# The down product of expert tiles as three products of high and low parts, made one tile later

## The chip, the cores and the metric

The kernel runs on one core of one Trainium2 chip, in one launch. The metric is the device time of that launch in microseconds (us), lower is better; a figure for a kernel is the median of its runs.

The engines of a core that matter here: TensorE (PE: matrix products; PEld is its weight loads, which overlap the products), VectorE (DVE), ScalarE (ACT), GpSimd (POOL) and SyncE (SP), which only issues transfers. Each works through its own list of instructions in order and stops at a semaphore until another engine, or a transfer that lands, has counted it up. So an instruction that waits holds back all that stands behind it on its engine.

## The reference, cut to what matters

A layer of four residual steps on 1024 tokens of 512 numbers, all in fp32: a state-space mixer, a mixture-of-experts block, a block-sparse product, and the same mixture-of-experts block again. Only the two expert blocks are touched:

```
g, u = split(x2 @ shared_w_gate_up.T);  shared_out = silu(g) * u @ shared_w_down.T
probs = softmax(x2 @ gate_w.T);  the best 2 of 16 experts per token, weights normed
gu  = einsum('th,eih->eti', x2, w_gate_up)      # 512 -> 2 * 128 per expert
act = silu(g) * u
out_e = einsum('eti,ehi->eth', act, w_down)     # 128 -> 512 per expert
out = sum over the 2 experts of out_e * combine + shared_out
```

## The kernel before, in words

The expert block runs twice (`run` 0 and 1). Each run computes the shared expert as two halves (`first`, `second`) over all tokens; between the two halves stands **the tile loop**, which this change is about. The 2048 pairs of token and expert are sorted by expert into slots, 128 slots to a tile. `TILES = 31` is the most tiles that any routing can need, and all 31 are always worked through. `own[tau]` in memory says which expert tile `tau` belongs to.

What one tile needs, by engine (names as the profile has them; a tile of memory may be seen under the name of the larger buffer that it lies in):

- SyncE loads gate and up weights (`tgu`, 512 KB, a ring of `GU_RING = 4`, seen as `mem<-wffn_d` L565) and down weights (`tdn`, 256 KB, a ring of `DN_RING = 3`, seen as `mem` or `spare<-wffn_d` L574). For both it first reads the expert's number from `own` into a register. It also stores the finished tile (`tile_out`, `slots_y<-quad`, 256 KB, L579).
- GpSimd gathers the tile's token rows (`cv<-xn_dram,toks`, L750), up to 256 KB; slots that are empty bring nothing.
- TensorE turns the rows (`t_rows`, L1917, 4 transposes), makes gate and up (`t_gate_up`, L1930, 8 products 128x128 by 128x128, plain fp32), and makes down (`t_down`, L1942, one product 128x128 by 128x512, plain fp32). The trace shows a plain fp32 product as two records.
- ScalarE takes the tanh of the gate (`t_tanh`, L1050), copies the turned rows out of PSUM (`t_rows_evac`, L1044) and copies the finished tile out of PSUM (`t_out`, `quad<-bank`, L1057), which counts up `ty_ok`.
- VectorE makes the hidden activations from tanh, gate and up (`t_hidden`, L1546 and L1548), into `thid`, a ring of `H_RING = 3`, seen as `E`.

The orders are written out by hand, one list to an engine, in steps of `k`. The list that matters most is SyncE's:

```
for k in range(TILES + 1):
    if k + GU_RING < TILES:
        tile_gate_up(run, k + GU_RING)
    if DN_RING <= k - 1 + DN_RING < TILES:
        tile_down(run, k - 1 + DN_RING)
    if k:
        tile_out(run, k - 1)
```

So in step `k` SyncE issues the gate-and-up load of tile `k+4`, the down load of tile `k+2`, and the store of tile `k-1`. The store waits for `ty_ok` of tile `k-1`.

Elsewhere (the mixer, the shared halves) products are already made from high and low parts: a value is copied to `fp32r`, a shorter form, as its high part, the difference goes to a second `fp32r` buffer, and `three` (L1627 through its helper) adds high by high, high by low and low by high in one bank. The buffers are `ah`, `al` for activations and `wh`, `wl` for weights.

Of the kernel before, what the change touches and what calls it, by code (L numbers as in the profile page):

```python
# [17 lines left out]
P = 128  # L18
TT = TOK // P
# [6 lines left out]
TILES = 2 * TOK // P + EXPERTS - 1  # L26
GU_RING, DN_RING, X_RING, Y_RING, H_RING = 4, 3, 4, 4, 3
# [6 lines left out]
def hybrid_layer(nc, x_d, wconv_d, wgate_d, wout_d, wdt_d, cpar_d, gpar_d, dtb_d, alog_d,  # L34
# [3 lines left out]
    ALU = mybir.AluOpType  # L38
    ACT = mybir.ActivationFunctionType
# [3 lines left out]
    with ctx:  # L43
        def sb(name, shape, dt=f32):
            return ctx.enter_context(nc.sbuf_tensor(name, shape, dt))

        def sem(name):
            return ctx.enter_context(nc.semaphore(name))
# [7 lines left out]
        wh = sb("wh", [P, 11, HID], f32r)  # L56
        wl = sb("wl", [P, 11, HID], f32r)
        ah = sb("ah", [P, 2, 4, P], f32r)
        al = sb("al", [P, 2, 4, P], f32r)
# [16 lines left out]
        thid = [E[:, 0, P * q:P * q + P] for q in range(H_RING)]  # L76
# [16 lines left out]
        tdn = [mem[:, 4096:4608], mem[:, 4608:5120], spare[:, HID:2 * HID]]  # L93
# [48 lines left out]
        bank = [ctx.enter_context(nc.psum_tensor(f"bank{n}", [P, HID], f32)) for n in range(8)]  # L142
# [65 lines left out]
        def counted(name, n):  # L208
            s = sem(name)
            per[name] = (s, n)  # L210
            return name
# [68 lines left out]
        dn_mm = counted("dn_mm", TT)  # L280
# [13 lines left out]
        td_in = [sem(f"td_in{q}") for q in range(DN_RING)]  # L294
        tx_in = [sem(f"tx_in{q}") for q in range(X_RING)]
        ty_out = [sem(f"ty_out{q}") for q in range(Y_RING)]
        ga_in = [sem(f"ga_in{t}") for t in range(TT)]
        tx_mm, tx_ok = sem("tx_mm"), sem("tx_ok")
        tg_mm, tg_th, tg_hg, tg_h = sem("tg_mm"), sem("tg_th"), sem("tg_hg"), sem("tg_h")
        ty_mm, ty_ok, cmb = sem("ty_mm"), sem("ty_ok"), sem("cmb")  # L300
        YB = (5, 6)
        DN_BANKS = ((4, 6, 7), (4, 5, 6, 7))

        def inc(instr, name, n=1):
            instr.then_inc(per[name][0], n)

        def now(eng, name, i, n):

            eng.wait_ge(per[name][0], per[name][1] * (i + 1) + n)

        def before(eng, name, i, n):

            eng.wait_ge(per[name][0], per[name][1] * i + n)
# [141 lines left out]
        def hidden_rows(i, j, low):  # L455
# [3 lines left out]
            s = (10, 0)[j - 2] if i % 2 else 7 + j  # L459
            return (wl if low else wh)[:, s, :].rearrange("p (a b) -> p a b", a=4)  # L460

        def job(run, tau):

            return run * TILES + tau

        def uses(ring, run, tau):

            return run * len(range(tau % ring, TILES, ring)) + tau // ring + 1
# [4 lines left out]
        def _(sp):  # L473
# [93 lines left out]

            def tile_down(run, tau):
                if tau >= DN_RING:
                    sp.wait_ge(ty_mm, job(run, tau - DN_RING) + 1)  # L570
                elif run:
                    sp.wait_ge(ty_mm, TILES)
                e = sp.value_load(own[0:1, tau:tau + 1], min_val=0, max_val=EXPERTS - 1)
                sp.dma_start(tdn[tau % DN_RING], experts[bass.ds(e, 1), :, 2, :].rearrange("e p n -> p (e n)")  # L574
                             ).then_inc(td_in[tau % DN_RING], 16)
# [216 lines left out]
        def _(act):  # L792
# [4 lines left out]
            def step(instr):  # L797
                steps[0] += 1
                instr.then_inc(act_step, 1)
                return steps[0]  # L800
# [168 lines left out]
            for b in range(BATCH):  # L969
                bs = slice(b * SEQ, (b + 1) * SEQ)  # L970
                act.wait_ge(pe_step, b + 1)
                n = step(nc.scalar.activation(v_hm[:, bs], bank[(DG, ST)[b]][:, :], ACT.Identity, bias=dtb[:, 0:1]))
                act.wait_ge(act_step, n)
                n = step(nc.scalar.activation(u_hm[:, bs], v_hm[:, bs], ACT.Abs))
# [53 lines left out]
            def hidden(i, j):  # L1028
                now(act, g_mm, i, j + 1)
                if j >= 2:  # L1030
                    now(act, a_lo, i, j - 1)
                else:
                    before(act, a_lo, i, 3 + j)
                inc(nc.scalar.activation(gt[:, j % 2, :], bank[j % 2][:, :], ACT.Tanh, scale=0.5), f_th)
                now(act, f_h, i, j + 1)
                before(act, dn_mm, i, TT)
                inc(nc.scalar.activation(hidden_rows(i, j, 0), gt[:, j % 2, :].rearrange("p (a b) -> p a b", a=4),
                                         ACT.Copy), a_hi)
# [7 lines left out]
            def t_tanh(run, tau):  # L1046
                act.wait_ge(tg_mm, job(run, tau) + 1)
                if tau >= H_RING:
                    act.wait_ge(ty_mm, job(run, tau - H_RING) + 1)
                nc.scalar.activation(thid[tau % H_RING], bank[2 + tau % 2][:, 0:P], ACT.Tanh,  # L1050
                                     scale=0.5).then_inc(tg_th, 1)

            def t_out(run, tau):
                act.wait_ge(ty_mm, job(run, tau) + 1)
                if tau >= Y_RING:
                    act.wait_ge(ty_out[tau % Y_RING], 16 * uses(Y_RING, run, tau - Y_RING))
                nc.scalar.activation(ybuf[tau % Y_RING], bank[YB[tau % 2]][:, :], ACT.Copy).then_inc(ty_ok, 1)  # L1057

            for run in range(2):
                if run == 1:  # L1060
                    layer_norm(2)
                    layer_norm(3)
                act.wait_ge(rt_dve, run * 3 + 2)
                nc.scalar.activation(pr[:, :, :], pr[:, :, :], ACT.Exp).then_inc(rt_dve, 1)
                first, second = 2 * run, 2 * run + 1
                act.wait_ge(rt_tr, run + 1)
                for j in range(4):
                    hidden(first, j)
                for k in range(-2, TILES + 1):
                    if 0 <= k < TILES:  # L1070
                        t_tanh(run, k)
                    if k + 2 < TILES:
                        t_rows_evac(run, k + 2)
                    if 0 <= k - 1:
                        t_out(run, k - 1)
                    if 1 <= k <= 4:
                        w_part(second, k - 1)
                    if run == 0 and 11 <= k <= 14:
                        if k == 11:
                            act.wait_ge(sp_ok, 1)  # L1080
                        nc.scalar.activation(wh[:, k - 5, :], wsp[:, k - 11, :], ACT.Copy).then_inc(sp_hi, 1)
                    if 20 <= k <= 21:
                        w_part(second, k - 16)
                for j in range(4):
                    hidden(second, j)
# [3 lines left out]
        def _(dve):  # L1089
# [11 lines left out]
            TS, STT, TTn = nc.vector.tensor_scalar, nc.vector.scalar_tensor_tensor, nc.vector.tensor_tensor  # L1101
# [277 lines left out]
            for run in range(2):  # L1379
# [162 lines left out]
                def t_hidden(tau):  # L1542
                    n = job(run, tau) + 1
                    dve.wait_ge(tg_th, n)
                    hid = thid[tau % H_RING]
                    STT(hid, hid, 1.0, bank[2 + tau % 2][:, 0:P], ALU.add, ALU.mult).then_inc(tg_hg, 1)  # L1546
                    dve.wait_ge(tg_hg, n)
                    TTn(hid, hid, bank[2 + tau % 2][:, P:2 * P], ALU.mult).then_inc(tg_h, 1)  # L1548

                first, second = 2 * run, 2 * run + 1  # L1550
                hidden_gate(first, 0)
# [66 lines left out]
        def _(pe):  # L1618
            mm = nc.tensor.matmul
            credit(pe, (big_mm, tr_mm, st_mm, off_mm, diag_mm, ss_mm, out_half, g_mm, u_mm, dn_mm))  # L1620

            def three(out, hi, lo, w_hi_, w_lo_, first, last, data_left):

                pairs = ((hi, w_hi_), (hi, w_lo_), (lo, w_hi_)) if data_left else \
                    ((w_hi_, hi), (w_hi_, lo), (w_lo_, hi))
                for n, (l, r) in enumerate(pairs):
                    got = mm(out, l, r, start=first and n == 0, stop=last and n == 2)  # L1627
                return got
# [174 lines left out]
            for run in range(2):  # L1803
# [33 lines left out]
                if run == 0:  # L1837
# [3 lines left out]
                       start=True, stop=True).then_inc(pe_step, 1)  # L1841
# [91 lines left out]
                    last.then_inc(tg_mm, 1)  # L1933

                def t_down(tau):
                    pe.wait_ge(tg_h, job(run, tau) + 1)
                    pe.wait_ge(td_in[tau % DN_RING], 16 * uses(DN_RING, run, tau))
                    if tau >= 2:
                        pe.wait_ge(ty_ok, job(run, tau - 2) + 1)
                    else:  # L1940
                        now(pe, dn_acc, 2 * run, TT)
                    mm(bank[YB[tau % 2]][:, :], thid[tau % H_RING], tdn[tau % DN_RING], start=True,  # L1942
                       stop=True).then_inc(ty_mm, 1)

                first, second = 2 * run, 2 * run + 1
                for n, (what, a, b) in enumerate(FFN_ORDER):
# [10 lines left out]
                        tokens()  # L1957
                for tau in range(2):
                    t_rows(tau)
                for k in range(TILES + 1):  # L1960
                    if k < TILES:
                        t_gate_up(k)
                    if k + 2 < TILES:
                        t_rows(k + 2)
                    if k:
                        t_down(k - 1)
                for what, a, b in FFN_ORDER:
                    if what == "gu":
                        gate_up(second, a, b, 0)
# [65 lines left out]
```

## Time and profile before

| | us |
|---|---|
| median of 3 runs | 2027.59 (2026.63 to 2031.39) |
| the profiled execution, its time | 2021.97 |
| its span, first to last instruction | 2020.1 |
| PE busy | 1966.5 (97%) |
| DVE busy | 1504.9 (74%) |
| ACT busy | 1181.0 (58%) |
| POOL busy | 1034.4 (51%) |
| mean granted clock of TensorE, full speed is 1 | 0.993 |

How to read it: a share of busy time is a mean over stages with different limits. The tile loop runs twice, from about 1669 to 1765 us and from about 1886 to 1981 us of the span. "idle before, releaser" is the time in which an engine stood still before an instruction, and what ended it. The clock 1.00 is 2.4 GHz, 0.50 is 1.2 GHz.

### The profile page before, as it was taken

The numbers are of one execution on the slowest core, as the hardware profiler recorded it, in microseconds if no ns is written. First come the engines' busy times: TensorE is split into PE (matmuls) and PEld (weight loads), VectorE is DVE, ScalarE is ACT, GpSimd is POOL, SyncE is SP. The second block draws the span as 40 slices with busy tenths as digits, with TensorE's granted clock in tenths as the row PEclk, the third lists the DMA queues.
The fourth block names the chain that finished last, engine by engine and source line by source line (L and its number), as shares of the span: only waits on it lengthen the run. The fifth ranks groups of instructions, "written<-read, shape, count | busy, mean of one in ns | idle before, by whom it ended". The sixth has DMA issues, their size and how long they took to land.

```text
span 2020.1 us, 38785 instructions
## 1 busy us (share of the span) xinstructions
PE 1966.5 (97%) x11776; PEld 1634.7 (81%) x11776; DVE 1504.9 (74%) x2838; ACT 1181.0 (58%) x2570; POOL 1034.4 (51%) x907
## 2 busy tenths in 40 slices
PE   5999999999999999999999999999999989998998
PEld 4888888888888888888888888888888868876887
DVE  7998599859976997699679967985899572176315
ACT  4785388538843874497449645963696335432442
POOL 1497059616941793279228823981497025250433
PEclk8999999999999999999999999999999999999999
DMA  2552145214512351334134313530352049931896
GB/s 101 160 169 56 49 120 168 57 45 121 162 47 74 111 147 43 92 113 127 43 92 135 111 38 97 150 101 28 107 162 83 21 138 379 340 114 42 310 378 199
DMA packets 143910, 253.95 MB, mean 126 GB/s; under 512 B 21448, under 2 KB 37832, under 8 KB 143696
## 3 DMA queue, kind: packets, MB, share of 16 engines
q1 hardware_dynamic: 134848, 231.35, 36.7%
q0 software_dynamic: 7520, 16.80, 2.7%
q10 hardware_dynamic: 1328, 3.15, 0.4%
q8 instruction: 111, 1.82, 0.4%
q14 instruction: 103, 0.84, 0.1%
HBM read 233.38 MB, written 25.69 MB: 128 GB/s over the span
## 4 chain that ended last, share of the span: by engine, by line
PE 90%; DVE 6%; ACT 1%; issue 1%; POOL 0%; DMA 0%; DVEq 0%; ACTq 0%; SPq 0%
PE bank L1627 60%; PE bank L1739 7%; PE bank L1930 6%; PE bank L1753 5%; PE bank L1693 4%; PE bank L1942 3%; PE bank L1721 2%; PE bank L1917 1%; DVE Y L1230 1%; DVE spare L1318 1%; PE bank L1712 1%; PE bank L1760 1%; PE bank L1635 1%; DVE Y L1239 1%; POOL wl L743 0%
## 5 line engine op out<-in xcount | busy, mean ns | idle before, releaser
L1627 PE MATMUL bank<-xh,wh 128*128 128x512 f32 x1288 | 523.4, 406 | 10.7 <-POOL wl L713 4.0
L1627 PE MATMUL bank<-xh,wl 128*128 128x512 f32 x1288 | 504.4, 392 | 0.0
L1627 PE MATMUL bank<-xl,wh 128*128 128x512 f32 x1288 | 502.2, 390 | 0.0
L713 POOL TENSOR_TENSOR wl<-raw,wh 128x512 fp32r<-128x512 f32 x144 | 192.8, 1344 | 460.8 <-ACT wh L861 460.8
L1230 DVE SCALAR_TENSOR_TENSOR Y<-bank,cpar,Y 128x511 f32<-128x511 f32 (+2 forms) x384 | 286.8, 747 | 24.4 <-ACT Y L905 15.4
L1627 PEld LDWEIGHTS bank<-xh,wh 128*128 128x128 f32 x1288 | 242.9, 189 | 60.6 <-POOL wl L713 4.9
L1627 PEld LDWEIGHTS bank<-xh,wl 128*128 128x128 f32 x1288 | 242.0, 188 | 54.2
L1627 PEld LDWEIGHTS bank<-xl,wh 128*128 128x128 f32 x1288 | 243.2, 189 | 45.5 <-issue 0.5
L730 POOL TENSOR_TENSOR Y<-Y,gt 128x512 f32<-128x512 f32 x128 | 184.9, 1444 | 94.5 <-DVE gt L1284 92.8
L1292 DVE TENSOR_TENSOR al<-Y,ah 128x512 fp32r<-128x512 f32 x128 | 95.6, 747 | 169.1 <-ACT ah L963 169.1
L1627 PE MATMUL bank<-wh,ah 128*128 128x512 f32 x544 | 213.7, 393 | 2.8 <-DVE X L1539 2.2
L1627 PE MATMUL bank<-wh,al 128*128 128x512 f32 x544 | 211.9, 389 | 0.0
L1627 PE MATMUL bank<-wl,ah 128*128 128x512 f32 x544 | 211.7, 389 | 0.0
L963 ACT ACTIVATE ah<-Y 128x512 fp32r<-128x512 f32 x128 | 80.6, 630 | 212.0 <-PE bank L1627 212.0
L937 ACT ACTIVATE gt<-bank 128x512 f32<-128x512 f32 x128 | 76.4, 597 | 165.7 <-PE bank L1627 97.9
L680 POOL TENSOR_TENSOR Y<-Y,E 128x384 f32<-128x384 f32 x128 | 136.3, 1065 | 44.6 <-DVE E L1261 44.6
L925 ACT ACTIVATE mem<-mem,hpt 128x128 f32<-128x128 f32 x512 | 156.2, 392 | 0.0
L905 ACT ACTIVATE Y<-bank,cpar 128x512 f32<-128x512 f32 x128 | 99.2, 775 | 96.3 <-PE bank L1627 95.4
L750 POOL DMA_INDIRECT cv<-xn_dram,toks x62 | 63.0, 1017 | 173.7 <-DVE own L1479 89.6
L706 POOL TENSOR_TENSOR mem<-mem,quad 128x512 f32<-128x512 f32 x112 | 143.7, 1307 | 0.0
L692 POOL TENSOR_TENSOR mem<-mem,hpt 128x384 f32<-128x384 f32 x128 | 107.3, 839 | 66.6 <-DVE mem L1198 61.3
L1546 DVE SCALAR_TENSOR_TENSOR E<-E,bank 128x128 f32<-128x128 f32 x62 | 17.8, 288 | 153.2 <-ACT E L1050 145.1
(232 smaller groups left out, 4072.0 us busy)
## 6 DMA issues: line engine op xcount, KB each, us to landing
mem<-c_rows SPq DMA_DIRECT2D x128, 256.0 KB, 3.8
mem<-wffn_d SPq DMA_DIRECT2D x62, 512.0 KB
E<-e_rows SPq DMA_DIRECT2D x256, 96.0 KB, 3.4
raw<-wconv_d SPq DMA_DIRECT2D x80, 256.0 KB, 3.0
cv<-c_rows SPq DMA_DIRECT2D x64, 256.0 KB, 3.9
spare<-c_rows SPq DMA_DIRECT2D x64, 256.0 KB, 4.2
raw<-wgate_d SPq DMA_DIRECT2D x64, 256.0 KB, 2.7
raw<-wout_d SPq DMA_DIRECT2D x64, 256.0 KB, 2.6
```

What stands on the lines that cost most here:

```text
L680: inc(pool.tensor_tensor(dst, dst, E[:, u % ER, :], ALU.add), y_ok)
L692: inc(pool.tensor_tensor(xd[:, u % 2, :, :].rearrange("p c (h d) -> p c h d", d=HD), xs[:, u % 3, 0:CH - 1, :].rearrange("p c (h d) -> p c ...
L706: inc(pool.tensor_tensor(L[n % LR], L[n % LR], G[:, b * CH:(b + 1) * CH, :].rearrange("p c i -> p (c i)"), ALU.mult), lg_ok)
L713: inc(pool.tensor_tensor(wl[:, W_SLOT[p], :], raw[:, R_SLOT[p], :], wh[:, W_SLOT[p], :], ALU.subtract), w_lo)
L730: inc(pool.tensor_tensor(dst, dst, gt[:, n % 2, :], ALU.mult), y_gated)
L905: inc(nc.scalar.activation(dst, bank[big_bank(i, k)][:, :], ACT.Identity, scale=cpar[:, tile, TAPS - 1:TAPS], bias=cpar[:, tile, TAPS:TAPS ...
L925: last = nc.scalar.activation(L[n % LR][:, c * P:(c + 1) * P], L[n % LR][:, c * P:(c + 1) * P], ACT.Relu, scale=-1.0, bias=hp[:, b * CH + ...
L1230: last = STT(dst[:, s:SEQ], bank[big_bank(i, k)][:, 0:SEQ - s], cpar[:, tile, TAPS - 1 - s:TAPS - s], dst[:, s:SEQ], ALU.mult, ALU.add)
L1627: got = mm(out, l, r, start=first and n == 0, stop=last and n == 2)
L1739: last = mm(b4(DG)[hs, c, :], xs[:, u % 3, c, hs], L[(2 * u + h) % LR][:, c * P:(c + 1) * P], start=True, stop=True)
L1753: last = mm(b4(OF)[:, c, :], S[:, u % 2, c, :], CT[:, t * P:(t + 1) * P], start=True, stop=True)
L1930: last = mm(bank[2 + tau % 2][:, a * P:(a + 1) * P], tgu[tau % GU_RING][:, a, kt * P:(kt + 1) * P], xT[tau % 2][:, kt, :], start=kt == 0, ...
```

## The change

The down product of a tile becomes three products of high and low parts, as elsewhere in the kernel. For this

- ScalarE copies the down weights of the tile to `ah` (`t_down_hi`) and the hidden activations to `wh` (`t_hid_hi`), both `fp32r`;
- VectorE subtracts these from the full values into `al` and `wl` (in `t_hidden`, counted by `td_lo` and `th_lo`);
- TensorE makes `t_down` of tile `k-2` in step `k`, where before it made that of tile `k-1`; ScalarE's `t_out` moves from tile `k-1` to tile `k-2` in step `k` likewise, behind the two new copies;
- SyncE's down load waits for `td_lo` in place of `ty_mm`. SyncE's order stays as it was.

```
+            def t_down_hi(run, tau):
+                act.wait_ge(td_in[tau % DN_RING], 16 * uses(DN_RING, run, tau))
+                if tau < 2:
+                    now(act, dn_mm, 2 * run, TT)
+                else:
+                    act.wait_ge(ty_mm, job(run, tau - 2) + 1)
+                nc.scalar.activation(down_rows(tau, 0), tdn[tau % DN_RING], ACT.Copy).then_inc(td_hi, 1)
+
+            def t_hid_hi(run, tau):
+                act.wait_ge(tg_h, job(run, tau) + 1)
+                nc.scalar.activation(hid_rows(tau, 0), thid[tau % H_RING], ACT.Copy).then_inc(th_hi, 1)
...
-                for k in range(-2, TILES + 1):
+                for k in range(-2, TILES + 2):
                     if 0 <= k < TILES:
                         t_tanh(run, k)
+                        t_down_hi(run, k)
+                        t_hid_hi(run, k)
                     if k + 2 < TILES:
                         t_rows_evac(run, k + 2)
-                    if 0 <= k - 1:
-                        t_out(run, k - 1)
+                    if 0 <= k - 2:
+                        t_out(run, k - 2)
...
                     TTn(hid, hid, bank[2 + tau % 2][:, P:2 * P], ALU.mult).then_inc(tg_h, 1)
+                    dve.wait_ge(td_hi, n)
+                    TTn(down_rows(tau, 1), tdn[tau % DN_RING], down_rows(tau, 0), ALU.subtract).then_inc(td_lo, 1)
+                    dve.wait_ge(th_hi, n)
+                    TTn(hid_rows(tau, 1), hid, hid_rows(tau, 0), ALU.subtract).then_inc(th_lo, 1)
...
                 def t_down(tau):
-                    pe.wait_ge(tg_h, job(run, tau) + 1)
-                    pe.wait_ge(td_in[tau % DN_RING], 16 * uses(DN_RING, run, tau))
+                    pe.wait_ge(th_lo, job(run, tau) + 1)
...
-                    mm(bank[YB[tau % 2]][:, :], thid[tau % H_RING], tdn[tau % DN_RING], start=True,
-                       stop=True).then_inc(ty_mm, 1)
+                    three(bank[YB[tau % 2]][:, :], hid_rows(tau, 0), hid_rows(tau, 1), down_rows(tau, 0),
+                          down_rows(tau, 1), True, True, True).then_inc(ty_mm, 1)
...
-                for k in range(TILES + 1):
+                for k in range(TILES + 2):
                     if k < TILES:
                         t_gate_up(k)
                     if k + 2 < TILES:
                         t_rows(k + 2)
-                    if k:
-                        t_down(k - 1)
+                    if k >= 2:
+                        t_down(k - 2)
...
                 if tau >= DN_RING:
-                    sp.wait_ge(ty_mm, job(run, tau - DN_RING) + 1)
+                    sp.wait_ge(td_lo, job(run, tau - DN_RING) + 1)
```

How it stands in ScalarE's list, before: a little over one step of the tile loop once its rings are full (`E<-bank` is the tanh, `hpt` or `spare<-bank` the turned rows, `quad<-bank` the finished tile, which counts up `ty_ok`).

```order
L1050 ACTIVATE E<-bank 128x128 [waits ty_mm,tg_mm]
L1044 ACTIVATE hpt<-bank 128x512 [waits tg_mm,tx_mm]
L1057 ACTIVATE quad<-bank 128x512 [waits ty_out1,ty_mm]
L1050 ACTIVATE E<-bank 128x128 [waits ty_mm,tg_mm]
L1044 ACTIVATE spare<-bank 128x512 [waits tg_mm,tx_mm]
L1057 ACTIVATE quad<-bank 128x512 [waits ty_out2,ty_mm]
```

And ScalarE's list of the change at the same place (`ah<-` is the copy of the down weights, `wh<-E` that of the hidden activations).

```order
L1059 ACTIVATE E<-bank 128x128 [waits th_lo,tg_mm]
L1068 ACTIVATE ah<-mem 128x512 [waits ty_mm,td_in1]
L1072 ACTIVATE wh<-E 128x128 [waits tg_h]
L1053 ACTIVATE spare<-bank 128x512 [waits tg_mm,tx_mm]
L1078 ACTIVATE quad<-bank 128x512 [waits ty_out1,ty_mm]
```

The wait for the down load (`td_in`) now stands on ScalarE, ahead of the copy that counts up `ty_ok`; before it stood on TensorE.

SyncE's list in the tile loop, of the change, from one store to the next (`slots_y<-quad` is the store, L571 and L580 read the expert's number).

```order
L586 DMA slots_y<-quad 128x512 [waits ty_ok]
L571 TENSOR_LOAD own [waits tg_mm]
L571 ISA x2
L572 ISA
L572 DMA mem<-wffn_d 128x2x512
L580 TENSOR_LOAD own [waits td_lo]
L580 ISA x2
L581 ISA
L581 DMA spare<-wffn_d 128x512
L586 DMA slots_y<-quad 128x512 [waits ty_ok]
```

Nothing moved in it; the down load waits for `td_lo` where it waited for `ty_mm`, and it still stands behind the store and the gate-and-up load.

## Rows read from the trace of the kernel before

**Rows 1.** Page: span, busy time by engine, clock and DMA share in 40 slices.

```profile
span 2020.1 us, 38785 instructions
...
PE 1966.5 (97%) x11776; PEld 1634.7 (81%) x11776; DVE 1504.9 (74%) x2838; ACT 1181.0 (58%) x2570; POOL 1034.4 (51%) x907
...
PEclk8999999999999999999999999999999999999999
DMA  2552145214512351334134313530352049931896
```

**Rows 2.** Chain that ended last, 1700 to 1712 us: start, duration, what.

```profile
1700.90 0.44 PE bank L1917 x4
1701.34 0.86 PE bank L1942 x2
1702.20 1.78 PE bank L1930 x16
1703.98 0.44 PE bank L1917 x4
```

**Rows 3.** Groups by line, 1668 to 1765 us: busy, mean ns, idle before.

```profile
L1942 PE MATMUL bank<-mem,E 128*128 128x512 f32 x42 | 21.7, 598 | 0.6 <-issue 0.4 <-DVE E L1548 0.2
L1057 ACT ACTIVATE quad<-bank 128x512 f32<-128x512 f32 x31 | 18.5, 597 | 9.6 <-PE bank L1942 9.6
...
L1942 PE MATMUL bank<-spare,E 128*128 128x512 f32 x20 | 10.2, 594 | 0.0
L1044 ACT ACTIVATE hpt<-bank 128x512 f32<-128x512 f32 x16 | 9.6, 597 | 11.4 <-PE bank L1917 11.2 <-issue 0.2
...
L1548 DVE TENSOR_TENSOR E<-E,bank 128x128 f32<-128x128 f32 x31 | 8.9, 287 | 1.1
L1050 ACT ACTIVATE E<-bank 128x128 f32<-128x128 f32 x31 | 8.6, 278 | 32.6 <-PE bank L1930 29.8 <-issue 2.8
...
L1019 ACT ACTIVATE wh<-raw 128x512 fp32r<-128x512 f32 x6 | 3.7, 622 | 0.0
```

**Rows 4.** Stretches of the loop: PE, PEld, DVE, ACT, POOL busy, clock, DMA.

```profile
1690.00:1720.00 30.00, 30.00 (x218) 25.56 (x218) 5.43 (x19) 16.24 (x34) 19.91 (x16) 1.00 1.04 396
1720.00:1750.00 30.00, 29.55 (x210) 24.70 (x209) 5.47 (x20) 15.35 (x31) 11.57 (x11) 1.00 1.04 385
1750.00:1765.00 15.00, 14.85 (x98) 11.59 (x98) 2.87 (x10) 6.21 (x14) 0.00 (x0) 1.00 0.72 262
```

**Rows 5.** Chain that ended last: a stretch of products of parts.

```profile
1660.63 7.14 PE bank L1627 x30
```

**Rows 6.** Page: VectorE's subtraction of a high part, 128x512.

```profile
L1292 DVE TENSOR_TENSOR al<-Y,ah 128x512 fp32r<-128x512 f32 x128 | 95.6, 747 | 169.1 <-ACT ah L963 169.1
```

**Rows 7.** Timeline of SyncE's queue, a little over one step.

```profile
1700.67 0.33 SPq L574 DMA_DIRECT2D spare<-wffn_d  x1
1701.05 0.43 SPq L579 DMA_DIRECT2D slots_y<-quad  x1
1702.23 0.38 SPq L565 DMA_DIRECT2D mem<-wffn_d  x1
1703.66 0.33 SPq L574 DMA_DIRECT2D mem<-wffn_d  x1
```

**Rows 8.** Page: DMA issues, KB each, median us from issue to landing.

```profile
spare<-c_rows SPq DMA_DIRECT2D x64, 256.0 KB, 4.2
raw<-wgate_d SPq DMA_DIRECT2D x64, 256.0 KB, 2.7
```

**Rows 9.** Timeline: a down load issued, and the product of that tile.

```profile
1726.37 0.34 SPq L574 DMA_DIRECT2D mem<-wffn_d  x1
...
1729.70 0.33 SPq L574 DMA_DIRECT2D spare<-wffn_d  x1
...
1732.60 1.10 PE L1942 MATMUL bank<-mem,E 128*128 128x512 f32 x2 [0.45 <-issue]
```

**Rows 10.** Stretches of 1 us outside the loop, columns as in rows 4.

```profile
1798.00:1799.00 1.00, 0.00 (x0) 0.00 (x0) 0.96 (x4) 0.00 (x0) 0.00 (x0) 1.00 0.00 0
1799.00:1800.00 1.00, 0.45 (x4) 0.45 (x5) 1.00 (x3) 0.93 (x2) 0.00 (x0) 1.00 0.00 0
1801.00:1802.00 1.00, 0.55 (x3) 0.55 (x4) 1.00 (x3) 0.55 (x2) 0.00 (x0) 0.73 0.00 0
1802.00:1803.00 1.00, 1.00 (x7) 1.00 (x5) 1.00 (x2) 0.40 (x1) 0.00 (x0) 0.50 0.00 0
1805.00:1806.00 1.00, 1.00 (x6) 0.84 (x5) 0.97 (x3) 1.00 (x3) 1.00 (x2) 1.00 0.00 0
```

More of the change, by code:

```diff
@@ L298, in hybrid_layer @@
         tx_mm, tx_ok = sem("tx_mm"), sem("tx_ok")
+        td_hi, td_lo, th_hi, th_lo = sem("td_hi"), sem("td_lo"), sem("th_hi"), sem("th_lo")
         tg_mm, tg_th, tg_hg, tg_h = sem("tg_mm"), sem("tg_th"), sem("tg_hg"), sem("tg_h")
@@ L460, in hidden_rows, with down_rows, hid_rows @@
             return (wl if low else wh)[:, s, :].rearrange("p (a b) -> p a b", a=4)
+        def down_rows(tau, low):
+            return (al if low else ah)[:, tau % 2, :, :].rearrange("p a b -> p (a b)")
+        def hid_rows(tau, low):
+            return (wl if low else wh)[:, 10, tau % 2 * P:(tau % 2 + 1) * P]
         def job(run, tau):
@@ L569, in tile_down @@
                 if tau >= DN_RING:
-                    sp.wait_ge(ty_mm, job(run, tau - DN_RING) + 1)
+                    sp.wait_ge(td_lo, job(run, tau - DN_RING) + 1)
                 elif run:
-                    sp.wait_ge(ty_mm, TILES)
+                    sp.wait_ge(td_lo, TILES)
                 e = sp.value_load(own[0:1, tau:tau + 1], min_val=0, max_val=EXPERTS - 1)
@@ L1035, in hidden @@
                 now(act, f_h, i, j + 1)
+                if i % 2:
+                    act.wait_ge(ty_mm, job(i // 2, TILES))
                 before(act, dn_mm, i, TT)
@@ L1048, in t_tanh @@
                 if tau >= H_RING:
-                    act.wait_ge(ty_mm, job(run, tau - H_RING) + 1)
+                    act.wait_ge(th_lo, job(run, tau - H_RING) + 1)
                 nc.scalar.activation(thid[tau % H_RING], bank[2 + tau % 2][:, 0:P], ACT.Tanh,
                                      scale=0.5).then_inc(tg_th, 1)
+            def t_down_hi(run, tau):
[8 more added lines that the diff above has]
+                nc.scalar.activation(hid_rows(tau, 0), thid[tau % H_RING], ACT.Copy).then_inc(th_hi, 1)
             def t_out(run, tau):
```

## The prediction

> **What bounds the kernel now.** I read the page first: TensorE is busy 97% of the span, and the digits of the DMA line are high in only two places [rows 1]. These two places are the tile loops, and only they are changed, so the rest of the kernel is taken as it was. Inside the loop I read the chain of work that ended last: it is TensorE alone, and it repeats 0.44 us of turned rows, 0.86 us of down product and 1.78 us of gate and up [rows 2]. That is **3.08 us a tile**, and the row of the next transposes (1703.98 against 1700.90) says the same. TensorE is busy 30.00 of 30 us there [rows 4]. So before, TensorE sets the loop. But the transfers are full as well: the DMA share is 1.04 at 396 and 385 GB/s, and drops to 0.72 only where no more loads are issued [rows 4]. ScalarE has room: it is busy 16.24 of 30 us, 1.7 of 3.08 a tile, and most of what it waits for is TensorE [rows 3, 4].
>
> Third, SyncE's queue. From a store (L579, 1701.05) to the next gate-and-up load (L565, 1702.23) it takes 1.18 us, to the next down load (L574, 1703.66) 2.61 us; from that down load to the one before (1700.67) it is 2.99 us [rows 7]. Hardly any of this is waiting: it is reading the expert's number and building the transfer. SyncE needs about 3.0 of the 3.08 us of a tile. It has no room for being held up.
>
> **The change part by part.** *TensorE.* A down product was 0.86 us [rows 2]. Thirty products of parts, 128x512, ran in 7.14 us, 0.238 each [rows 5], so three are 0.71 and a tile's work on TensorE falls to 2.93 us, by 0.15. The Trainium skill, "FP8 and Floating Point Precision", TensorE Precision Notes, has true fp32 as four passes through the array; by that, three passes in place of four would save a quarter, 0.21 us a tile. It changes nothing in what follows, where TensorE does not set the pace.
>
> *ScalarE.* Two copies come: 128x512 to `fp32r` at 0.62 (as L1019), and 128x128 at 0.28 (as L1050) [rows 3]. With tanh 0.28, rows 0.60 and out 0.60 a tile is 2.38 us: under 2.93, so ScalarE is no bound by its work.
>
> *VectorE.* A subtraction 128x512 at 0.75 [rows 6] and one of 128x128 at 0.29 [rows 3] join 0.58 us: 1.6 us a tile, no bound.
>
> *The waits.* This is what decides. ScalarE's `t_down_hi(k)` now waits for the down load of tile k, and `t_out(k-2)`, which counts up `ty_ok`, stands behind it in the same step. SyncE's store of tile k-2 waits for that `ty_ok`, and behind the store stand the gate-and-up load of k+4 and the **down load of k+2**. That load in turn is what ScalarE waits for two steps later. The store of tile k used to be released in ScalarE's step k+1; now it is in step k+2, but SyncE's order was not moved with it. So there is a ring over two steps:
>
> - ScalarE, from the landing of the down load to `ty_ok`: 0.62 + 0.28 + 0.60 + 0.60 = 2.10 us [rows 3];
> - SyncE, from the store to the issue of the down load: 2.6 us [rows 7];
> - the transfer, from issue to landing: not shown by itself for this load. From below, a load of 256 KB where the transfers are lightly used lands 2.7 us after issue; another kind of 256 KB takes 4.2 [rows 8]. From above, in the loop: the load issued at 1726.37 is that of the product at 1732.60, which waited 0.45 us for something that no engine had left open (the other load, issued at 1729.70, is the next tile's). That is 6.2 us [rows 9], at a DMA share of 1.04. After the change the same bytes move in some 4.5 us in place of 3.08, so the share falls to about 0.7, that of the end of the loop [rows 4]. I take 4.2, between the two ends and nearer the light one, since 512 KB were issued 1.4 us ahead on the same queue;
> - three hand-overs by semaphore (landing to ScalarE, to SyncE, SyncE to its queue): 0.2 us, an estimate.
>
> The sum is 2.1 + 2.6 + 4.2 + 0.2 = 9.1 us for two steps, **4.55 us a tile** against 3.08. It is TensorE that then waits, for `th_lo` and the rows that ScalarE gives out late.
>
> The Trainium skill, "DMA: Bandwidth & Descriptors", Anatomy of one DMA, fits a transfer that GpSimd issues as about 2.0 us plus its bytes at 436 GB/s. For 256 KB that is an estimate of 2.6 us, and the ring would be 7.5 us and the tile 3.75. The 6.2 us of the loop before disagree, since loads queue there.
>
> *How many tiles.* The down loads of tiles 0 to 2 are issued ahead of the loop, that of 3 ahead of the first store. Tiles 4 to 30 are bound: 27 a run. In the last two SyncE has no gate-and-up load to issue (1.2 us less), but the last product now comes about as much later behind ScalarE's copies: even. So 27 x (4.55 - 3.08) = 39.7 us a run, **79 us** for two. The profiled execution took 1.9 us more than its span, 2022.0 in all; 2022.0 + 79 = 2101. The median of the runs shown is 5.6 us above that execution, so on their scale it is 2027.6 + 79 = **2107 us**, 3.9% slower.
>
> TensorE's saving of 0.15 x 62 = 9 us lies under the ring and gives nothing. Other SyncE waits are no issue: `td_lo` of k-1 is long counted when the load of k+2 comes up, and the gate-and-up load has a ring of four and over two steps to land.
>
> *Bounds.* With a landing of 2.7 us the ring is 7.6, the tile 3.8, and the sum 27 x 0.72 x 2 = 39 us: 2066. With 6.2 us it is 11.1, 5.55 and 133 us: 2161.
>
> **Rivals.**
>
> 1. *Short landing.* The light share lets the load land in 2.7 to 3.3 us: 2066 to 2083. For it: the 2.7 of [rows 8]. Against it: the 512 KB just ahead, and gathers. The fit on the DMA page of the Trainium skill is on this side. Chance 0.17, and 0.04 for something shorter still, 2034 to 2066.
> 2. *Long landing, or a slow clock.* TensorE will now stand still for up to 2 us at a time. Outside the loop, after two slices of 1 us with TensorE busy 0.00 and 0.45, the granted clock fell from 1.00 to 0.50, that is from 2.4 to 1.2 GHz [rows 10]. If the whole loop ran at 1.2 GHz, TensorE would need 2 x 2.93 = 5.9 us a tile, above the ring, and the loss would be 2.8 x 27 x 2 = 150 us: 2178. Against it: a loop that is full at 1.2 GHz gives the clock no reason to stay there (at 1802 to 1803 TensorE was busy 1.00, and at 1805 the grant was 1.00 again [rows 10]), and a spell of a few us costs less than the 3 us that TensorE has over in two steps. With a landing above 5.2 us this side is 2134 to 2175. Chance 0.12.
> 3. *Faster: no ring.* If the down load still lands before ScalarE asks for it, TensorE stays the bound at 2.93 us: 2027.6 - 9 = 2018. It decides at the point where the ring comes under two tiles of TensorE, 5.9 us; 2.1 + 2.6 + 0.2 alone are 4.9, so the load would have to land within 1.0 us of its issue. The shortest 256 KB shown takes 2.7 [rows 8]. It can only be if ScalarE's or SyncE's list is not held as I read it. Chance 0.06.
> 4. *Same.* The ring is missing and SyncE's own 3.0 us, or the full transfers, take TensorE's gain: 2022 to 2033. Chance 0.03.
>
> **How the numbers follow.** The likeliest case, a landing of 3.3 to 5.2 us, gives 2083 to 2134 and has 0.58. The range of 2060 to 2150 takes in it, rival 1 and the near half of rival 2, and leaves out about 0.19. A difference of 0.3%, 6 us, is about what a measurement of this kernel can tell from no change. Faster 0.06, same 0.03, slower 0.91.
>
> **What would show it.** In the profile of the changed kernel each tile loop is some 40 us longer. TensorE is busy some 65% of it and the DMA share falls from 1.04 to about 0.7. ScalarE's `ah<-mem` and `ah<-spare` (L1068) have the longest idle time before them in the loop, 1.5 us a tile or more, with a transfer (or nothing that shows) as releaser. SyncE's stores (L586) wait for `quad` L1078 in every step, and a down load (L581) follows its store by 2.6 us. Tiles come in pairs, a long and a short one, since the ring goes over two steps. The rest of the kernel is as long as before. I am wrong if stores are issued without a wait, if L1068 never waits for its load, or if the clock line shows 0.5 through the loop.

## The result and the profile after

The changed kernel takes **2092.84 us** (2087.6 to 2095.91, 4 runs) against 2029.49 of the kernel before in the same comparison. The ratio is 1.0314 with a 95% interval of 1.0296 to 1.0332: 3.1% slower, +63 us. The prediction was 3.9%, +79 us on the same base, with a range that holds the result.

The span of the profiled execution is 2090.5 us, 70.4 more than [rows 1]. First, the page: busy time of the engines, the clock and the DMA share in 40 slices.

```profile
span 2090.5 us, 39219 instructions
...
PE 1983.0 (95%) x11838; PEld 1653.1 (79%) x11838; DVE 1554.3 (74%) x2962; ACT 1213.1 (58%) x2694; POOL 1034.2 (49%) x907
...
PEclk8999999999999999999999999999999999999999
DMA  2552135124313530352144134313520498614984
```

VectorE is 49 us busier than in [rows 1] and ScalarE 32, both well below the span: the added time is waiting. The stretches of the loop show whose (columns as in [rows 4]):

```profile
1690.00:1720.00 30.00, 23.70 (x179) 20.67 (x178) 11.15 (x30) 14.93 (x38) 13.53 (x10) 1.00 0.89 294
1720.00:1750.00 30.00, 21.15 (x153) 17.78 (x152) 9.99 (x27) 15.31 (x38) 11.55 (x11) 1.00 0.89 284
```

TensorE was busy 30.00 and 29.55 of 30 us in [rows 4]; now it is 23.70 and 21.15. The transfers are slower too, 294 GB/s for 396. ScalarE is busy half the time. All of them wait, so none of them is the bound by its work; what they wait for has to be read. The view of one line's instructions shows what ScalarE's new copy of the down weights (L1068) waits for, over both runs (us, times):

```profile
  DMA mem<-wffn_d: 76.6, 36
  DMA spare<-wffn_d: 32.7, 16
  PE bank L1654: 2.9, 3
```

That is 109 us in 52 of 62 tiles, for the down load. And SyncE's waits show its store (L586) behind ScalarE's out (L1078):

```profile
SPq L586 <- ACT quad L1078: 88.4, 56, 3.3
```

In the kernel before, the same wait was `SPq L579 <- ACT quad L1057: 8.8, 6, 2.3`. The chain that ended last, once round the ring (start, duration, what), of the kernel after:

```profile
1704.76 0.25 issue
1705.01 0.29 ACT wh L1072
1705.30 0.48 ACT hpt L1053
1705.79 0.49 ACT quad L1078
1706.30 0.33 SPq L586
...
1707.42 0.39 SPq L572
...
1708.75 0.06 SPq L581
...
1708.91 3.96 DMA mem<-wffn_d
...
1713.43 0.29 ACT wh L1072
1713.72 0.48 ACT hpt L1053
1714.21 0.50 ACT quad L1078
1714.72 0.33 SPq L586
...
1716.97 3.88 DMA mem<-wffn_d
```

Read it as a circle: out (L1078) counts up `ty_ok`, the store (L586) follows in 0.02 us, then the gate-and-up load (L572) and the down load (L581) are issued, the down weights land 3.96 us later, and ScalarE's copies lead to the next out. From the landing at 1712.87 to the store at 1714.72 is 1.85 us; from store to load 2.61 us (1706.30 to 1708.91) or 2.25 (1714.72 to 1716.97); the transfer is 3.9 to 4.0. Together 8.0 to 8.4 us, for two tiles. (In this and other kernels single loads differ; where sizes are compared below, the median of the down loads is used that stand in the chain between 1685 and 1765 and between 1935 and 2015 us. Here it is 4.07 us, of 18.) TensorE, which was the whole chain in [rows 2], does not stand in this cut. It does not vanish from the chain altogether: from 1722 to 1738 the view takes it through four steps of TensorE (gate and up, rows, down) and ScalarE. In these steps L1068 still waited 1.6 to 2.2 us for its load, and tiles came every 4.1 to 4.3 us, so the ring of loads is as long there.

The timeline of ScalarE gives the pace, by the starts of L1068 (the first line is tile 3, the last tile 30):

```profile
1682.76 0.63 ACT L1068 ACTIVATE ah<-mem 128x512 fp32r<-128x512 f32 x1 [0.97 <-DMA mem<-wffn_d]
1688.16 0.63 ACT L1068 ACTIVATE ah<-mem 128x512 fp32r<-128x512 f32 x1 [2.92 <-DMA mem<-wffn_d]
1691.01 0.63 ACT L1068 ACTIVATE ah<-spare 128x512 fp32r<-128x512 f32 x1 [0.37 <-DMA spare<-wffn_d]
1696.21 0.63 ACT L1068 ACTIVATE ah<-mem 128x512 fp32r<-128x512 f32 x1 [3.23 <-DMA mem<-wffn_d]
1699.54 0.63 ACT L1068 ACTIVATE ah<-mem 128x512 fp32r<-128x512 f32 x1 [1.37 <-DMA mem<-wffn_d]
...
1793.42 0.63 ACT L1068 ACTIVATE ah<-mem 128x512 fp32r<-128x512 f32 x1 [1.80 <-DMA mem<-wffn_d]
```

The first steps alternate, 5.4, 2.85, 5.2, 3.3 us, since the ring goes over two steps and odd and even tiles are two chains; between 1717 and 1742 us the steps are even, 3.9 to 4.4 us. From tile 3 to tile 30 it is 110.7 us, **4.10 us a tile** against 3.08.

### The profile page after: what moved, and what is told of

It reads as the page before. It is cut to its first block, busy times and chain, and to the rows that moved or that the text cites. A ratio compares the mean times of both kernels' runs of the same rounds, so it can differ in the third digit from the quotient of the medians.

```text
span 2090.5 us, 39219 instructions
## 1 busy us (share of the span) xinstructions
PE 1983.0 (95%) x11838; PEld 1653.1 (79%) x11838; DVE 1554.3 (74%) x2962; ACT 1213.1 (58%) x2694; POOL 1034.2 (49%) x907
## 4 chain that ended last, share of the span: by engine, by line
PE 80%; DVE 6%; DMA 5%; ACT 3%; issue 3%; SPq 2%; another core or an unknown queue 0%; DVEq 0%; POOL 0%; ACTq 0%
PE bank L1654 59%; PE bank L1766 6%; PE bank L1780 5%; PE bank L1720 4%; DMA mem<-wffn_d 3%; PE bank L1748 2%; DMA spare<-wffn_d 2%; DVE Y L1253 1%; PE bank L1957 1%; DVE spare L1341 1%; PE bank L1739 1%; PE bank L1787 1%; PE bank L1662 1%; SPq L580 1%; SPq L572 1%
## 5 line engine op out<-in xcount | busy, mean ns | idle before, releaser
L1241 DVE SCALAR_TENSOR_TENSOR mem<-mem,hpt,bank 128x64 f32<-128x64 f32 x512 | 121.0, 278 | 9.1
```

The lines of the kernel that those rows point to most:

```text
L1241: last = STT(S[:, u % 2, c, hs], S[:, u % 2, c - 1, hs], hp[:, b * CH + c, 3, 2 * pair + h:2 * pair + h + 1], so[:, c, hs], ALU.mult, ALU.add)
```

## The experiments

Eleven kernels ran, in three groups; each is compared with the kernel before on the same chip (its median was 2030.6, 2026.1 and 2027.6 us in the three).

**SyncE's store one step later.** The change moved the store's release by one step and left SyncE's list. Here the list follows.

```
-                for k in range(TILES + 1):
+                for k in range(TILES + 2):
...
-                    if k:
-                        tile_out(run, k - 1)
+                    if k >= 2:
+                        tile_out(run, k - 2)
```

> The changed kernel, with SyncE's store moved one step later too (tile k-2 in step k). Theory 'ring' (load of the down weights -> ScalarE's copy -> out -> store -> next down load, over two steps, 8.3 us): the ring now goes over three steps, 8.3 to 9.7 us by whether a load takes 4.0 or 5.5 us, so 2.93 (TensorE) to 3.2 us a tile, and the time is 2020 to 2038 us. Rival 'copies': ScalarE's and VectorE's added work slows the loop by itself; then the time stays at 2085 or more. Rival 'late load': the down weights are now wanted two steps before the product and a ring of 3 buffers with full transfers can't bring them; then the tile stays above 3.6 us, 2057 us or more.

Measured: 2036.81 us, ratio 1.0029 (1.0010 to 1.0047). Three numbers in SyncE's list take back 57 of the 63 us, and the result lies in the ring's range. ScalarE's and VectorE's added work is all still there, so the rival "copies" falls, and so does "late load" in the form in which it was given. The store's waits are down to a third:

```profile
SPq L586 <- ACT quad L1078: 29.9, 31, 2.2
```

**The store two steps later.** The same edit with 3 in place of 2.

> The changed kernel, with SyncE's store two steps later (tile k-3 in step k). Theory 'ring': the ring goes over four steps and can't bind; what is left is TensorE at 2.93 us, SyncE at about 3.0, or the transfers at 1.25 MB over 0.4 MB/us, 3.1 us: 2018 to 2031 us, no slower than with one step. Rival 'late load': 2057 us or more, as with one step. Rival 'copies': 2085 or more.

Measured: 2029.38 us, ratio 0.9996 (0.9985 to 1.0008): level with the kernel before, and the best form with the full loads. A stretch of its loop:

```profile
1690.00:1720.00 30.00, 28.52 (x215) 25.37 (x214) 16.55 (x36) 20.48 (x50) 19.65 (x16) 1.00 1.03 383
```

The DMA share is back at 1.03, and TensorE still waits 1.5 of 30 us.

**The down load first.** The store stays where the change has it; in a step SyncE issues the down load ahead of the gate-and-up load.

```
+                    if DN_RING <= k - 1 + DN_RING < TILES:
+                        tile_down(run, k - 1 + DN_RING)
                     if k + GU_RING < TILES:
                         tile_gate_up(run, k + GU_RING)
-                    if DN_RING <= k - 1 + DN_RING < TILES:
-                        tile_down(run, k - 1 + DN_RING)
```

> The changed kernel, with SyncE issuing the down load ahead of the gate-and-up load in a step; the store stays where it was. Theory 'ring': from store to down load it is 1.1 us in place of 2.25, and 512 KB less stand in front of the load, so it lands in 3.2 to 4.0 us: the ring is 6.2 to 7.0 us, 3.1 to 3.5 us a tile, 2030 to 2052 us. Rival 'copies': no change, 2085 to 2100. Rival 'late load': a load that is issued 1.1 us earlier gains 1.1 us in each step at most once, so 2075 or more.

Measured: 2069.19 us, ratio 1.0185 (1.0160 to 1.0209). The sign was right, the size was not, and 2069 is outside what any of the three had said. The chain shows which term was off:

```profile
1719.33 0.33 SPq L586
...
1720.43 0.33 SPq L581
```

and its next loads:

```profile
1712.42 5.06 DMA mem<-wffn_d
...
1724.51 4.50 DMA mem<-wffn_d
```

SyncE's term shrank as expected, from 2.25 or 2.6 us to 1.1. The transfer did not get shorter; it got longer: the median is 4.50 us, of 12, for 4.07. The expectation had "512 KB less in front of the load". That holds within a step, but the gate-and-up load of the step before still stands in front, as these rows of the timeline show (the first four are tile 21, the last three tile 29, behind which no gate-and-up load follows):

```profile
1745.79 0.38 SPq L572 DMA_DIRECT2D mem<-wffn_d  x1
1749.81 0.33 SPq L581 DMA_DIRECT2D mem<-wffn_d  x1
1750.91 0.38 SPq L572 DMA_DIRECT2D mem<-wffn_d  x1
1752.47 0.63 ACT L1068 ACTIVATE ah<-mem 128x512 fp32r<-128x512 f32 x1 [0.53 <-DMA mem<-wffn_d]
...
1775.20 0.38 SPq L572 DMA_DIRECT2D mem<-wffn_d  x1
1776.86 0.33 SPq L581 DMA_DIRECT2D spare<-wffn_d  x1
1781.79 0.63 ACT L1068 ACTIVATE ah<-spare 128x512 fp32r<-128x512 f32 x1 [2.17 <-DMA spare<-wffn_d]
```

Tile 21's load, 4.0 us behind the last gate-and-up load and with the next one 1.1 us behind it, landed within 2.66 us. Tile 29's, 1.66 us behind a gate-and-up load and with none behind it, took 4.93. Over both loops, among the loads that ScalarE waited for and that have the next gate-and-up load 0.9 to 1.6 us behind them, those issued at most 2.0 us after one have a median of 4.9 us (18 loads), those issued 3.0 us or more after one 3.1 us (13 loads). So the landing goes with how closely a large load stands ahead.

**Out first.** SyncE's list is untouched; on ScalarE the out of tile k-2 moves ahead of the wait for the down load of tile k.

```
                     if 0 <= k < TILES:
                         t_tanh(run, k)
+                    if 0 <= k - 2:
+                        t_out(run, k - 2)
+                    if 0 <= k < TILES:
                         t_down_hi(run, k)
...
-                    if 0 <= k - 2:
-                        t_out(run, k - 2)
```

> The changed kernel, with ScalarE's out of tile k-2 moved ahead of the copy of the down weights of tile k; SyncE's order is untouched. Theory 'ring': the store no longer stands behind the wait for the load. The way round is then over four steps: turned rows and product 1.15, out 0.7, SyncE 2.25, load 4.0 to 5.5, copies and rows 1.5, gate and up 1.8, together 11.4 to 12.9 us, 2.93 to 3.2 us a tile: 2020 to 2038 us. Rival 'copies': ScalarE does the same work, so 2085 or more. Rival 'late load': SyncE issues the load no earlier than the store lets it, 2057 or more.

Measured: 2044.49 us, ratio 1.0061 (1.0038 to 1.0084). The same work on every engine, in another order on ScalarE alone, gives back 49 us. It is 6 us above the range. The loads in its chain have a median of 4.75 us, of 14, inside what was assumed, so the missing 6 us are another term, which I have not found.

**A control: half the gate-and-up load, kernel before.** To free the transfers without touching a wait, the load of gate and up brings the gate half alone.

```
-                sp.dma_start(tgu[tau % GU_RING], experts[bass.ds(e, 1), :, 0:2, :].rearrange("e p k n -> p (e k) n")
+                sp.dma_start(tgu[tau % GU_RING][:, 0:1, :], experts[bass.ds(e, 1), :, 0:1, :].rearrange("e p k n -> p (e k) n")
```

> The kernel before, but each tile's gate-and-up load brings only the gate half (256 KB in place of 512; the up weights in the buffer are whatever was there, so that part of the computation is not done with its own weights). A control. If TensorE alone sets the loop before, 3.08 us a tile, nothing changes: 2024 to 2034 us. If the full transfers held it back, it gets faster by more than 6 us.

Measured: 2020.72 us, ratio 0.9973 (0.9958 to 0.9988): 5.4 us faster, below the range and short of the 6 us that the other reading asked for. The loop shows little of it: its chain is TensorE alone, with 3.08 us from one gate and up to the next.

```profile
1691.76 1.78 PE bank L1930 x16
1693.54 0.44 PE bank L1917 x4
1693.98 0.86 PE bank L1942 x2
1694.84 1.78 PE bank L1930 x16
```

and the two profiled spans differ by 0.5 us (2020.6 and 2020.1). From the first gate and up to the last, the two loops together are 186.4 us for 188.2, so full transfers cost the kernel before some 2 us in that pair of executions. Where the timed runs gain the rest of the 5 us is open.

**The half load in the changed kernel.**

> The changed kernel with the same half load (only the gate half of the gate and up weights is brought). Theory 'ring, and its transfer term is queueing': the down load lands 0.65 us sooner (256 KB less ahead of it at 0.4 MB/us), 3.3 us after issue; the ring is 7.5 us, 3.75 a tile, 2060 to 2072 us. Rival 'ring, but the transfer term is a fixed latency': 2088 to 2096, as with the full load.

Measured: 2066.05 us, ratio 1.0199 (1.0173 to 1.0225). This is as the ring with a queueing transfer term says. A turn of its chain:

```profile
1709.61 0.33 SPq L586
...
1711.80 2.89 DMA mem<-wffn_d
```

The store to the load is 2.2 us as before, the transfer 2.9 us here and 3.28 in the median of 17, for 4.07. A fixed latency would have left it. (Some of the gain may be the one that the control has too, and that is not explained.)

**The half load with the store two steps later.**

> The changed kernel with the store two steps later (tile k-3 in step k) and the same half load. Theory 'the transfers eat what the shorter products give': freed of them TensorE sets the pace at 2.93 us a tile, 0.15 x 62 = 9 us under the kernel before: 2017 to 2024 us. Rival 'SyncE's own 3.0 us a tile': 2024 to 2030. Rival 'ScalarE, 2.4 us and its hand-overs': as with the full load, 2026 to 2032.

Measured: 2018.89 us, ratio 0.9960 (0.9943 to 0.9976), in the range. But the control had gained 5.4 of these 7.2 us already, so the median alone says little of the product. The first and last gate-and-up products (the view of one line) say more. Of the control:

```profile
L1930 PE MATMUL bank<-hpt,mem x512: 272/275/377, 1670.8 to 1980.1; 128*128 128x128 f32 x171
```

and of this kernel:

```profile
L1957 PE MATMUL bank<-hpt,mem x512: 270/275/377, 1672.1 to 1976.0; 128*128 128x128 f32 x171
```

309.3 against 303.9 us over both loops and what lies between them: 5.4 us, of the 9 that 62 shorter products could give. Its down product takes what was worked out, in the chain:

```profile
1690.70 0.71 PE bank L1654 x3
```

**Lateness alone.** The kernel before, with TensorE's down product and ScalarE's out one tile later, and nothing else: one plain fp32 product, TensorE waits for the load.

```
-                for k in range(TILES + 1):
+                for k in range(TILES + 2):
...
-                    if k:
-                        t_down(k - 1)
+                    if k >= 2:
+                        t_down(k - 2)
```

(and `t_out(run, k - 2)` for `t_out(run, k - 1)` in ScalarE's list.)

> The kernel before with the lateness alone: TensorE makes the down product of tile k-2 in step k and ScalarE's out follows it; the product stays one plain fp32 product, no copies, TensorE itself waits for the down load, SyncE's order is untouched. Theory 'ring': the store's release does not stand behind the wait for a load, TensorE wants the load of k+2 only in its step k+4, so the way round has two steps more and stays under TensorE's 3.08 us: 2024 to 2034 us. Rival 'lateness alone is enough, since SyncE's list holds the loads back': 2045 or more.

Measured: 2030.47 us, ratio 1.0013 (0.9998 to 1.0027). SyncE's list is as wrong for this order as for the change, and it costs at most 0.3%.

**Lateness and the wait.** To this one line is added, on ScalarE behind the tanh. There are no copies and no subtractions.

```
                         t_tanh(run, k)
+                        act.wait_ge(td_in[k % DN_RING], 16 * uses(DN_RING, run, k))
```

> The kernel before with the lateness (as in the run with the lateness alone, one plain fp32 product, no copies, no subtractions) and one thing more: ScalarE waits for the down load of tile k in step k, behind the tanh and ahead of the rows and the out. Theory 'ring': this wait is the whole cause. The way round is 0.58 + 0.49 and a hand-over on ScalarE, 2.25 on SyncE and 4.0 of transfer, 7.4 us for two steps, 3.7 a tile: 54 x 0.62 = 33 us above before, 2050 to 2070 us. Rival 'copies': without them the loop stays where it was, 2024 to 2036.

Measured: 2076.12 us, ratio 1.0230 (1.0190 to 1.0269): +48 us from a wait in front of no new work. It is 6 us above the range, since the transfer took longer than the 4.0 us assumed. Its ring, from the chain:

```profile
1723.80 0.10 issue
...
1724.27 0.60 ACT quad L1057
1724.89 0.33 SPq L579
...
1727.19 4.86 DMA mem<-wffn_d
```

1.14 us on ScalarE, 2.3 on SyncE, 4.86 of transfer (the median of 20 is 4.85): 8.3 us for two tiles in this turn, hardly less than with the copies. The chain picks the longer loads here. Over all 52 loads of tiles 3 to 28 that ScalarE waited for, from issue to the end of the wait, the median is 4.3 us, for 4.1 in the changed kernel counted the same way. And from the first gate and up to the last the loop takes 115.7 us, for 121 with the copies and 94 in the kernel before. So of the 0.7 us by which ScalarE's part is shorter the ring keeps about half (2 x 5.5 / 30 = 0.4 us); the transfer gives back some 0.2.

**Why the down load first gained little.** The run with the down load first, with the half load as well.

> The changed kernel with the down load ahead of the gate-and-up load on SyncE, and the gate-and-up load halved (256 KB, the gate half alone is brought). It asks why the run with the down load first gained only 24 us. Theory 'shared engines': transfers issued behind a load slow it as those ahead do, so the half load takes 0.65 us off the ring again, as it did with the load ahead: 0.33 a tile, 2048 to 2056 us. Rival 'queue': what is issued behind does not matter; then the half load gives nothing here, 2064 to 2072.

Measured: 2055.51 us, ratio 1.0122 (1.0083 to 1.0161), just within the range of "shared engines". Against the kernel before of its group it is +27.9 us, where the down load first alone was +38.6: 10.7 us off, with an interval of several us. The same 256 KB less in the changed kernel took off 23.3 (63.3 to 40.0). From the first gate and up to the last, both loops together, the two steps are nearer: 17.0 us (223.2 to 206.2) and 20.6 (242.3 to 221.7). The median of the loads in the chain is 4.17 us, of 16, for 4.50.

This does not show that a load is slowed by what is issued behind it. The half load takes 256 KB away behind each down load, but also ahead of the next one, and the rows of the run with the down load first show how much depends on what stands closely ahead. The rival "queue" said that the half load would give nothing; it had left out the load of the step before, and so it falls only in that form. The two readings are not separated by these runs.

**Both edits on SyncE.**

> The changed kernel with the store two steps later and the down load ahead of the gate-and-up load. Without the ring of the store the next way round is that of the three buffers: load 5.3 us, copy 0.64, subtraction 0.75, SyncE until the issue 1 to 2.4, together 7.7 to 9.1 us for three tiles. Theory: SyncE's part shrinks, the way round falls under TensorE's 2.93 us a tile: 2019 to 2028 us. Rival 'transfers are full': no better than with the store alone, 2026 to 2032.

Measured: 2029.92 us, ratio 1.0012 (0.9989 to 1.0036). Not better than the store alone, as the rival "transfers are full" said. No version with full loads was found that beats the kernel before. Whether the full transfers hold these versions by their share, or through the way round of the three buffers of down weights, was not separated.

## Why the prediction was right

- **What bounded before.** TensorE at 3.08 us a tile, with the transfers full beside it: the control keeps the 3.08 with half of the largest load gone, so TensorE did set the loop. Full transfers cost it little: 1.8 us over both loops in the profiled pair. The timed runs gained 5 us, for a reason that stays open in the main.
- **The ring.** Its mechanism was right, and it is shown from four sides: by the chain, by taking the store out of it (57 us back), by taking the wait out of its way on ScalarE (49 us back), and by adding that wait alone to a kernel without copies (+48 us). Lateness without the wait costs at most 0.3%. The pieces, forecast and measured: ScalarE 2.1 and hand-overs 0.2, measured 1.85 in all, since ScalarE starts an instruction before the last one's end (the rows at 0.48 and 0.49 us in the chain for 0.58 to 0.60 busy); SyncE 2.6, measured 2.25 to 2.6 and mostly 2.3, so the 2.61 of [rows 7] is more than it mostly takes; transfer 4.2, measured 4.07 in the median. The sum was 9.1 and is 8.0 to 8.4; the tile 4.55 and is 4.10. 54 x 0.45 = 24 us of loss were forecast too much there.
- **What came near by luck.** The loss itself is only 16 us under the forecast (63 for 79), since 8 us are lost outside tiles 4 to 30, where the prediction had called the end of the loop even. In the two profiled executions the loops, first gate and up to last, are 54.1 us longer, the stretches behind them 6.9 and 6.7, and what stands ahead 2.7. Behind each loop TensorE now waits for low parts that VectorE makes (`wl`), 8.1 us in all where it was 0.2. Behind the first loop:

```profile
PE bank L1654 <- DVE wl L1575: 2.3, 1, 2.3
PE bank L1654 <- DVE wl L1551: 2.3, 1, 2.3
```

The 4.2 us of the transfer are in part luck too: they were picked between 2.7 and 6.2, with a fall of the DMA share to 0.7 as one reason, and that fall did not come.
- **The worth of the shorter product.** 0.71 us was right: 0.15 less than the 0.86 of the plain product, and not a quarter less. That it would give nothing under the ring was right. Without the ring it still gives nothing with full loads (0.9996), and 5.4 of 9 us with the half load, so the transfers take it; this was rival 4's mechanism, there without the ring.
- **The DMA share.** Forecast 0.7, measured 0.89 at 294 GB/s. This step failed: I had scaled the share with the bytes per time. At [rows 4] 262 GB/s were 0.72 in a stretch in which the loads had ended, so the share is not the bytes alone. TensorE was forecast busy some 65% of the loop and is at 75% over the two stretches, as the tile is shorter.
- **The rivals.** Short landing: the median was 4.07 us in the changed kernel, 3.28 with 256 KB less ahead of the load, 4.50 with the down load first. The fit of "DMA: Bandwidth & Descriptors" in the Trainium skill (Anatomy of one DMA), which is given for a transfer that GpSimd issues and makes an estimate of 2.6 us for 256 KB, is not what this load does. The slow clock: it stayed at 1.00 in both stretches above, though TensorE stood still for 21 to 30% of them. In the second loop, outside these stretches, it fell to 0.50 three times, near 2004, 2021 and 2042 us, for some 3 us each, and each time a slice of 1 us in which TensorE stood still was shortly ahead. The first of them (columns as in [rows 4]):

```profile
2001.00:2002.00 1.00, 0.00 (x0) 0.00 (x0) 0.00 (x0) 0.58 (x2) 0.69 (x1) 1.00 0.79 291
2004.00:2005.00 1.00, 1.00 (x6) 1.00 (x6) 0.12 (x2) 0.75 (x3) 0.00 (x0) 0.50 0.70 262
```

That the second loop is 2.9 us longer than the first (122.6 and 119.7) may be this, which is not shown; it is small beside the ring.

## What to carry to other kernels

When one step of a hand-written pipeline is moved later, follow its release on every queue: a store that waits in an in-order queue holds back the loads behind it, and if the releasing engine in turn waits for such a load, the round trip sets the pace however idle the engines are. Look for the wait that was moved in front of a release, count how many steps the way round spans, and divide. A list of engines that all wait, with none at its bound, is the sign in the profile.

## What was not expected of the hardware

- Moving a 256 KB load ahead of the 512 KB load of its step did not make it land sooner: 4.50 us for 4.07. The 512 KB load of the step before stands in front of it instead. Issued at most 2.0 us behind that one, it took 4.9 us in the median (18 loads), and 3.0 us or more behind it 3.1 (13 loads), with the next 512 KB load 0.9 to 1.6 us behind it in both groups. Whether a load issued behind adds anything is not shown.
- The time from issue to landing moves against the pace of the ring: with 0.7 us less of other work in the ring (1.14 for 1.85 on ScalarE) the load took 4.3 for 4.1 us in the median of all that ScalarE waited for, and 4.85 for 4.07 among those in the chain. A term that is queueing gives back a part of what is saved elsewhere in the ring.
- Reading an expert's number and issuing a transfer costs SyncE 1.1 to 1.2 us a load: from the store at 1714.72 to the down load at 1716.97, with one other load between.
